# Feed-forward block and router of a PixArt layer on unsplit fp32 operands instead of three products of split ones

## What is computed

```python
x = x + xcond(layernorm(x), cond, ctx)        # below
x = x + moe(layernorm(x), wqkv, w1, w2)       # 8 experts, top 2

# xcond, with x the normed input
h1 = adaln(x, t, norm1);  x = mha(h1, h1) + x        # 16 heads of 64
h2 = adaln(x, t, norm2);  x = mha(h2, context) + x
h3 = adaln(x, t, norm3)
u = h3 @ ff_w1 + ff_b1                               # 128 -> 1024
a, gate = split(u)
x = (a * gelu(gate)) @ ff_w2 + ff_b2 + x             # 512 -> 128

# router of moe, on the normed x
q, k, v = split(x @ wqkv.T)                          # 3 x 8 numbers per position
logits = sum_j softmax(q_e * k_j) * v_j              # then top 2 of 8
```

## Time and profile before

| | us |
|---|---|
| median of 3 runs | 2328.56 |
| lowest, highest | 2327.22, 2332.91 |
| the profiled execution, its own time | 2332.13 |
| its span in the trace | 2330.4 |
| PE busy | 2128.4 (91%) |
| DVE, ACT, POOL busy | 1267.6 (54%), 1277.4 (55%), 820.5 (35%) |

### The profile page before, as it was taken

One profiled execution on the slowest core, in us unless ns is written; L12 is line 12 of the kernel. 1 busy time (PEld: TensorE's weight loads), 2 busy tenths in 40 slices (PEclk: granted clock), 3 DMA queues, 4 the chain that ended last, 5 costly groups with the idle time before them and its releaser, 6 DMA issues. The chain is left out here.

```text
span 2330.4 us, 39202 instructions
## 1 busy us (share of the span) xinstructions
PE 2128.4 (91%) x11308; PEld 1392.0 (60%) x11309; DVE 1267.6 (54%) x3228; ACT 1277.4 (55%) x2453; POOL 820.5 (35%) x1024
## 2 busy tenths in 40 slices
PE   4899999999999999999999999999998457998986
PEld 4555666666666666666666666666655235776764
DVE  3454656565666656565756565666555243444454
ACT  3565666565666666666666666666655133443432
POOL 1222323424332433333333424332323234445443
PEclk8999999999999999999999999999998668999998
DMA  4112212112122122121212112121111311221255
GB/s 126 41 28 50 50 41 50 51 47 63 38 58 55 45 57 61 46 50 46 50 49 51 46 51 63 40 55 50 55 38 36 103 32 42 54 56 53 72 171 164
DMA packets 145566, 135.93 MB, mean 58 GB/s; under 512 B 15562, under 2 KB 117482, under 8 KB 145451
## 3 DMA queue, kind: packets, MB, share of 16 engines
q1 hardware_dynamic: 136170, 116.42, 18.7%
q0 software_dynamic: 9280, 18.28, 2.3%
HBM read 90.82 MB, written 40.67 MB: 56 GB/s over the span
## 5 line engine op out<-in xcount | busy, mean ns | idle before, releaser
L1582 POOL TENSOR_TENSOR pr<-pr,sm 128x512 f32<-128x512 f32 x256 | 263.2, 1047 | 770.9 <-DVE sm L1198 770.9
L676 PE MATMUL ps<-tt,V 128*128 128x512 f32 x1024 | 503.7, 597 | 4.4 <-ACT tt L930 4.4
L930 ACT ACTIVATE kp<-ps 128x512 f32<-128x512 f32 x512 | 296.1, 600 | 201.1 <-PE ps L266 176.7
L1188 DVE TENSOR_REDUCE mx<-ps 128x8 f32<-128x512 f32 x256 | 176.9, 691 | 339.7 <-PE ps L629 336.5
L658 PE MATMUL ps<-pt,h_tm 64*128 64x256 f32 x2048 | 291.5, 404 | 2.1 <-ACT pt L930 2.1
L629 PE MATMUL ps<-kp,hf 128*64 128x256 f32 x2048 | 277.0, 392 | 5.6 <-ACT kp L930 2.8
L930 ACT ACTIVATE tt<-ps 128x512 f32<-128x512 f32 x512 | 274.1, 588 | 4.9 <-PE ps L658 4.9
L266 PE MATMUL ps<-hk,M 128*128 128x512 f32 x768 | 252.0, 451 | 27.0 <-DVE pr L1191 24.9
L266 PE MATMUL ps<-cT,M 128*128 128x512 f32 x768 | 267.5, 471 | 0.0
L676 PEld LDWEIGHTS ps<-tt,V 128*128 128x128 f32 x1024 | 184.5, 191 | 98.9 <-issue 71.7
L930 ACT ACTIVATE pt<-ps 128x512 f32<-128x512 f32 x256 | 153.6, 600 | 152.2 <-PE ps L641 149.9
(11 more groups left out here) (219 smaller groups left out, 2993.1 us busy)
## 6 DMA issues: line engine op xcount, KB each, us to landing
mod<-emb_s SPq DMA_DIRECT2D x96, 256.0 KB, 4.3
xr<-rows_s SPq DMA_DIRECT2D x144, 66.0 KB
cb<-y_s SPq DMA_DIRECT2D x32, 256.0 KB, 5.7
x_in<-in_x_dram SPq DMA_DIRECT2D x16, 256.0 KB, 4.4
xn_s<-x_in SPq DMA_DIRECT2D x16, 256.0 KB, 2.1
h_tm<-h_tm SPq DMA_DIRECT2D x32, 128.0 KB
res<-xn_s SPq DMA_DIRECT2D x16, 256.0 KB, 2.8
c_in<-in_ctx_dram SPq DMA_DIRECT2D x16, 256.0 KB, 4.5
```

The lines of the kernel that those rows point to most:

```text
L676: mm = nc.tensor.matmul(psO[:], Vw[a][:, g * HG + h, :], tt[:, h % 2, h // 2, :], start=(g == 0 and h == 0), stop=(g == 1 and h == HG - 1))
L930: return nc.scalar.activation(o, i, ACT.Copy)
L1188: nc.vector.tensor_reduce(mx[:, p % 2, :], heads(psS[p % 2][:]), AX_X, ALU.max).then_inc(max_done, 1)
L1582: tensor(v, v, sm[:, p, :].unsqueeze(2).broadcast_to([P, HG, 64]), ALU.mult).then_inc(prob_done, 1)
```

## The change

The feed-forward part and the router use float32 operands, each stored once. Every `mm3` of theirs becomes one float32 matmul. W1 and W2 are loaded straight into place, so that their copies and subtractions are gone, and SP waits for two steps less. WR is copied half by ACT and half by DVE. h3 has one copy, made by ACT; `ln_lo` remains for norm 1 alone (`ln1_lo`). gelu writes into gl instead of tmp, DVE multiplies in place there, and the two splitting steps are gone. gl has two places, taken in turn by f; gelu of slice f waits for `f2_done` of two slices before. Waits on tmp by the feed-forward part are gone. The space of phase A shrinks, and the gap `skip` of phase B with it. Expert weights, attention and phase B are as they were.

```diff
@@ -122,9 +122,9 @@
...
-            W1 = sa("W1", [P, 2, 2 * DFF], F32R)
-            W2 = sa("W2", [P, 2, FT, D], F32R)
-            WR = sa("WR", [P, 2, 3 * E], F32R)
+            W1 = sa("W1", [P, 2 * DFF])
+            W2 = sa("W2", [P, FT, D])
+            WR = sa("WR", [P, 3 * E])
@@ -144,10 +144,10 @@
...
-                h3 = sw("h3", [P, 2, CT], F32R)
+                h3 = sw("h3", [P, CT])
...
-                gl = sw("gl", [P, 2, CT], F32R)
+                gl = sw("gl", [P, 2, CT])
@@ -160,8 +160,6 @@
...
-                raw1 = sg("raw1", [P, 2 * DFF])
-                raw2 = sg("raw2", [P, FT, D])
@@ -174,7 +172,7 @@
...
-            skip = sbb("skip", [P, 6750])
+            skip = sbb("skip", [P, 5190])
@@ -233,7 +231,7 @@
...
-        ff_done, gel, glu, glu_hi, glu_lo = sem("ff_done"), sem("gel"), sem("glu"), sem("glu_hi"), sem("glu_lo")
+        ff_done, gel, glu = sem("ff_done"), sem("gel"), sem("glu")
@@ -338,8 +336,8 @@
...
-                  ((2, 2, "back2", y2_done), (4, 3, "ln4", hx_lo[3]), (7, 3, "router", mix_cp)),
-                  ((2, 2, "ln3", hx_lo[2]), (6, -1, "ln1", hx_lo[0])),
+                  ((2, 2, "back2", y2_done), (4, 3, "ln4", hx_hi[3]), (7, 3, "router", mix_cp)),
+                  ((2, 2, "ln3", hx_hi[2]), (6, -1, "ln1", hx_lo[0])),
@@ -359,14 +357,8 @@
...
-            if u == 0 and ok(i - 3):
-                return [(glu_lo, FT * (i - 2))]
...
-            if u == 2 and ok(i - 2):
-                return [(st_u, 16 * (i - 1))]
-            if u == 3 and ok(i - 2):
-                return [(glu_lo, FT * (i - 2) + 1)]
@@ -387,14 +379,14 @@
...
-            sp.dma_start(raw1[:], t_in["L0_xcond_ff_w1"]).then_inc(ld_m, 16)
-            sp.dma_start(raw2[:], t_in["L0_xcond_ff_w2"].rearrange("(t p) n -> p t n", p=P)).then_inc(ld_m, 16)
+            sp.dma_start(W1[:], t_in["L0_xcond_ff_w1"]).then_inc(ld_m, 16)
+            sp.dma_start(W2[:], t_in["L0_xcond_ff_w2"].rearrange("(t p) n -> p t n", p=P)).then_inc(ld_m, 16)
...
-            sp.wait_ge(su_act, NSU + 2)
-            sp.wait_ge(su_dve, NSU + 2)
+            sp.wait_ge(su_act, NSU)
+            sp.wait_ge(su_dve, NSU)
@@ -697,17 +689,17 @@
...
-                    mm = mm3(bank[:], lambda k: W1[:, k, col:col + P], lambda k: h3[:, k, :])
+                    mm = nc.tensor.matmul(bank[:], W1[:, col:col + P], h3[:], start=True, stop=True)
...
-                pe.wait_ge(glu_lo, FT * c + f + 1)
-                mm3(psM[:], lambda k: W2[:, k, f, :], lambda k: gl[:, k, :], first=f == 0, last=f == FT - 1).then_inc(f2_done, 1)
+                pe.wait_ge(glu, FT * c + f + 1)
+                nc.tensor.matmul(psM[:], W2[:, f, :], gl[:, f % 2, :], start=f == 0, stop=f == FT - 1).then_inc(f2_done, 1)
...
-                    mm = mm3(psM[:, t * 3 * E:(t + 1) * 3 * E], lambda k: h3[:, k, t * P:(t + 1) * P], lambda k: WR[:, k, :])
+                    mm = nc.tensor.matmul(psM[:, t * 3 * E:(t + 1) * 3 * E], h3[:, t * P:(t + 1) * P], WR[:], start=True, stop=True)
@@ -828,7 +820,7 @@
...
-                        pe.wait_ge(hx_lo[2], i - 1)
+                        pe.wait_ge(hx_hi[2], i - 1)
@@ -942,15 +934,13 @@
...
-                    op = copy(WR[:, 0, :], ps[:, 0:3 * E])
+                    op = copy(WR[:, 0:E], ps[:, 0:E])
...
-            copy(W1[:, 0, :], raw1[:]).then_inc(su_act, 1)
-            copy(W2[:, 0], raw2[:]).then_inc(su_act, 1)
@@ -999,25 +989,17 @@
...
-                if k != 1:
-                    copy((hk if k == 0 else h3)[:, 0, :], psM[:]).then_inc(hx_hi[k], 1)
+                if k == 0:
+                    copy(hk[:, 0, :], psM[:]).then_inc(hx_hi[k], 1)
+                if k >= 2:
+                    copy(h3[:], psM[:]).then_inc(hx_hi[k], 1)
...
-                if f == 0:
-                    for w in tmp_free(c + 2, 2):
-                        act.wait_ge(*w)
-                if f > 0:
-                    act.wait_ge(glu_lo, n)
+                if not (isinstance(n, int) and n < 2):
+                    act.wait_ge(f2_done, n - 1)
...
-                nc.scalar.activation(tmp2, psS[1][:], ACT.Gelu, bias=b_1[:, FT + f:FT + f + 1]).then_inc(gel, 1)
-
-            def glu_split(c, f):
-                n = FT * c + f
-                act.wait_ge(glu, n + 1)
-                if not (isinstance(n, int) and n < 1):
-                    act.wait_ge(f2_done, n)
-                copy(gl[:, 0, :], tmp2).then_inc(glu_hi, 1)
+                nc.scalar.activation(gl[:, f % 2, :], psS[1][:], ACT.Gelu, bias=b_1[:, FT + f:FT + f + 1]).then_inc(gel, 1)
@@ -1082,7 +1064,7 @@
...
-                         2: ((3, 2, lambda c: ln_hi(c, 2)), (5, 2, lambda c: glu_act(c, 0)), (6, 2, lambda c: glu_split(c, 0)),
+                         2: ((3, 2, lambda c: ln_hi(c, 2)), (5, 2, lambda c: glu_act(c, 0)),
@@ -1092,8 +1074,6 @@
...
-                        if h in (3, 5, 7):
-                            glu_split(i - 2, h // 2)
@@ -1167,17 +1147,12 @@
...
-                    op = tensor(WR[:, 1, :], ps[:, 0:3 * E], f32(WR[:, 0, :]), ALU.subtract)
+                    op = nc.vector.tensor_copy(WR[:, E:], ps[:, E:3 * E])
...
-            dve.wait_ge(su_act, NSU + 1)
-            tensor(W1[:, 1, :], raw1[:], f32(W1[:, 0, :]), ALU.subtract).then_inc(su_dve, 1)
-            dve.wait_ge(su_act, NSU + 2)
-            tensor(W2[:, 1], raw2[:], f32(W2[:, 0]), ALU.subtract).then_inc(su_dve, 1)
-
@@ -1241,10 +1216,9 @@
...
-            def ln_lo(c, k):
-                dve.wait_ge(hx_hi[k], 2 * c + 2 if k == 0 else c + 1)
-                dst = hk if k == 0 else h3
-                tensor(dst[:, 1, :], psM[:], f32(dst[:, 0, :]), ALU.subtract).then_inc(hx_lo[k], 1)
+            def ln1_lo(c):
+                dve.wait_ge(hx_hi[0], 2 * c + 2)
+                tensor(hk[:, 1, :], psM[:], f32(hk[:, 0, :]), ALU.subtract).then_inc(hx_lo[0], 1)
@@ -1296,11 +1270,7 @@
...
-                nc.vector.scalar_tensor_tensor(tmp2, psS[0][:], b_1[:, f:f + 1], tmp2, ALU.add, ALU.mult).then_inc(glu, 1)
-
-            def glu_split_lo(c, f):
-                dve.wait_ge(glu_hi, FT * c + f + 1)
-                tensor(gl[:, 1, :], tmp2, f32(gl[:, 0, :]), ALU.subtract).then_inc(glu_lo, 1)
+                nc.vector.scalar_tensor_tensor(gl[:, f % 2, :], psS[0][:], b_1[:, f:f + 1], gl[:, f % 2, :], ALU.add, ALU.mult).then_inc(glu, 1)
@@ -1455,14 +1425,12 @@
...
-                         1: ((3, 2, after_attn2), (4, 2, stats3), (5, 3, lambda c: ln_lo(c, 3)), (6, 2, norm3), (8, -1, ln1_stats)),
-                         2: ((2, 3, router_sum), (4, 3, router_dot), (3, 2, lambda c: ln_lo(c, 2)), (4, -1, ln1), (6, 2, lambda c: glu_mul(c, 0)), (7, 2, lambda c: glu_split_lo(c, 0)), (8, -1, lambda c: ln_lo(c, 0)), (8, 3, top_first)),
+                         1: ((3, 2, after_attn2), (4, 2, stats3), (6, 2, norm3), (8, -1, ln1_stats)),
+                         2: ((2, 3, router_sum), (4, 3, router_dot), (4, -1, ln1), (6, 2, lambda c: glu_mul(c, 0)), (8, -1, ln1_lo), (8, 3, top_first)),
...
-                    if u == 3 and ok(i - 2) and h in (4, 6, 8):
-                        glu_split_lo(i - 2, h // 2 - 1)
@@ -1477,7 +1445,7 @@
...
-            ln_lo(0, 0)
+            ln1_lo(0)
```

## The result

The changed kernel takes **2346.2 us** (median of 6 runs, 2340.23 to 2348.12) where the kernel before takes 2327.89 (6 runs, 2321.72 to 2332.91). The ratio is 1.008, with a 95% interval of 1.0066 to 1.0093: 0.8% slower, as forecast (2347.1). The profiled execution took 2346.36 us, with a span of 2344.6.

The account below looks back on a forecast made before the run. PE's own stream was taken to bound the loop; 25.0 + 4.2 - 5.9 - 1.6 - 0.7 - 2.5 = +18.5 us took the median of 2328.56 to 2347.1 us, 0.8% slower, range 2337 to 2359.

Parts of the forecast that it names:

- What bounds the loop: Hardware loop: PE's own stream, 107.4 of 109.45 us a round; records count in full, sparing ACT and DVE counts nothing.
- The unit price, +0.16: Each 512-column up or down product: one float32 product at 0.86 us replaces three float32r records at 0.70.
- The router (-0.42): Routers 0 to 13 in PE's stream: 8 records at 0.92 us replace 12 at 1.34; -5.9 us in all.
- the start (-2.5): Start: SP stores emb without waiting for the two extra splitting steps; all that follows comes 2.5 us earlier.
- the router of chunk 15 (-1.6): Last router, nothing beside it: 0.9 us less for eight records at the low clock, plus the subtraction on h3 gone.
- Together +4.2: Feed-forward of chunks 13 and 14: +3.8 for 24 products, +1.7 for the low clock, -1.3 for waits gone in round 16.
- -0.7: Last chunk's feed-forward, round 17: products +2.0, subtraction on gl gone -1.3, ACT's last copy gone -1.4.
- my upper bound of 10.4: Last rounds: all eight splitting pairs of chunks 14 and 15 count at 1.3 us, not 4.0; rival 2341 us, chance 0.07.
- The clock falls more often: Rival, loop: four more falls to the lower clock at a mean of 2.6 us, +10, giving 2357 us; chance 0.13.
- The other rivals: Split records at half float32, 2357 (0.04); slot 3 wait goes, 2320 (0.05); all pairs count, 2341 (0.07); no change (0.02).
- The wait of slot 3: Rival: PE's 2.06 us wait before slot 3's first key goes, saving up to 2.06 x 13 = 26.8 us, 2320; chance 0.05.
- new wait for the gelu: Loop: gelu of slice f waits for the down product of f-2; bounded by nothing and 0.5 us a round.

Follow-up runs that it names:

- doubling: Up products issued twice, in the kernel before and in the kernel after: 2417.32 and 2442.18 us (one run each; kernel before on that chip 2302.91).
- the square: Four kernels, float32r or float32 products, each with or without splitting steps: 2326.80 and 2316.83 us with float32r, 2351.96 and 2346.20 with float32.
- a_resplit: Kernel after with the splitting steps put back into an unread buffer, PE waiting for them: 2351.96 us, ratio 1.0115 to the kernel before.
- b_three_pass: Kernel before without splitting steps on h3 and gl, three float32r records kept, gl in two places: 2316.83 us, ratio 0.9964.
- b_up_twice: Kernel before with both products of every up step issued twice: 2417.32 us (one run), kernel before on that chip 2302.91.
- b_router_twice: Kernel before with every router matmul issued twice, 12 more split records a chunk: 2358.91 us, ratio 1.0138.

## Why the prediction held, and where it did not

- **What bounds the loop: right.** DVE and ACT lost 62.5 and 39.8 us of work, the loop gained at most 0.14 us a round from it, and each record counted in full.
- **The unit price, +0.16: right.** Three measurements agree: 0.86 in the trace, 0.86 less 0.705 by doubling, and the sides of the square (1.48 and 1.52 for the forecast 1.50). A round without falls grew by 1.38. The 0.12 less than 1.50 is a part that the prediction did not have: in slot 2, from V to V around the first up step, before the change 3.14 us (1684.63 to 1687.77) and afterwards 3.26 (1705.89 to 1709.15), +0.12 for a pair that should cost +0.32. That is 0.20 less in one place, of which the square ties 0.10 to 0.14 a round to removing the splitting steps.
- **The router (-0.42), the start (-2.5), the router of chunk 15 (-1.6): right.** Measured -0.45 in place, -2.49 at the store, and -1.6 from the rows of chunk 15 to its counts. After the change that last router reads:

```profile
1927.57 1.90 PE L702 MATMUL ps<-WR,h 128*128 128x24 f32 x8 [0.69 <-ACT h L922]
```

- **The last rounds: the step that failed.** "Together +4.2" for chunks 13 and 14 and "-0.7" for the last chunk took 4.0 us for the shorter chain. It is worth 9.2 (a_resplit against after) to 11.8 (before against b_three_pass) in single traces, and some 4.5 to 8 by the medians. The mechanism was right and its size was not: in the slot shown above 1.3 was counted and 3.0 came, because the chain was waited for twice (0.7 and 1.0), and less waiting also brought time at the high clock (1.3). How large the gain is in a usual execution stays open between 4.5 and my upper bound of 10.4.
- **The clock: a rival that came in part.** "The clock falls more often" had 0.13 and a price of 10 us for four more falls. Four more there were behind the wait, 8.9 us in place of 4.5, and the first round, with its own, added 1.3: +5.7 in all. I had priced a further fall at 2.6, the mean of two, one of which was twice as long, and had left the first round out. The sign that I had named for it, clock values under 1.00 in more than two stretches of the loop, came. These are the falls of one execution of each kernel; what made them more frequent in this one was not shown.
- **The sum: right with two misses that cancel.** For the two traces: 18.5 + 5.0 (the loop) - 6.6 (last rounds) - 2.4 (phase B) = 14.5, and the profiled executions are 14.2 apart. The medians differ by 18.3, with 15 to 22 as the interval. How close the figure of 2347.1 came is luck; the terms of the steady rounds are not. In the 5.0 up to the last turn the falls (+5.7) and 0.12 in each of 12 rounds (-1.4) leave 0.7, and that stands in and behind round 15: from the router of chunk 12 to the last turn the difference grows by 3.9 us where 3.2 was forecast.
- **The other rivals fell.** The wait of slot 3 stayed at 2.06 us. Its reason against it was right too: the work ahead of the fourth maximum is the counting, and moving just that took 1.4 us from every round. PE shows no new wait for the gelu in the loop.
- **Open:** the 2.4 us of phase B, which are no more than the ten traces named above differ by in that phase (367.2 to 375.2 us, the two here 373.9 and 371.5); the difference between the chips; and what decides in which rounds the clock falls.

## What to carry to other kernels

Where the matrix engine is the bound, count its records and multiply by the distance between starts of each kind, between like neighbours: replacing three float32r records (0.70 us) by one float32 matmul (0.86) loses with 512 columns, and wins with 24 (1.34 or 1.36 against 0.92), where the number of records counts. Work taken off engines that nobody waits for is worth nothing in the steady rounds, yet in the fill and drain of a pipeline the steps of the chain pay, and can pay more than their own length (3.0 us for 1.3 in the slot shown). Before a wait is moved, look at what is late behind it: moving PE's wait gave nothing, moving five small steps of DVE that made it gave 1%.

## What was unexpected of the hardware

- The clock falls behind one and the same 2.06 us wait in some rounds and not in others, mostly for 3.4 us, at 1.4 to 1.6 us each. In one execution each there are 2 such falls at a round of 109.01 us, 2 at 110.37, 6 at 110.39, one in every round from 4 to 14 at 111.11 and at 114.42, and 8 at 117.24. With the wait at 0.66 us there is none up to round 14, in three kernels. New float32 records are not needed for it (b_up_twice).
- The clock can also fall without any wait of PE: in b_router_twice six times, right behind 24 records of 24 columns that take 2.60 us.
- At the low clock a float32 product of 512 columns takes 1.78 us, a little more than twice the 0.86 of the high clock.
- With 24 columns a record costs 0.113 us as float32r and 0.114 as float32, so that the exchange there is one of numbers alone, 12 against 8.
